# Grouped cross attention of a decoder: one pipeline over sixteen half sequences, with split float32r products

## The reference

```python
q = (x @ Wq).reshape(B, S, 16, 128)          # x: 8 x 256 x 512, Wq: 512 x 2048
k = (ctx @ Wk).reshape(B, S_enc, 4, 128)     # ctx: 8 x 256 x 512, Wk, Wv: 512 x 512
v = (ctx @ Wv).reshape(B, S_enc, 4, 128)
q = rms_norm(q, q_norm_w)                    # per head, eps 1e-6
k = rms_norm(k, k_norm_w)
k, v = repeat(k, 4), repeat(v, 4)            # four query heads share a key head
scores = einsum('bqhd,bkhd->bhqk', q, k) / 128 ** 0.5
out = einsum('bhqk,bkhd->bqhd', softmax(scores), v)
x = layernorm(x + out.reshape(B, S, 2048) @ Wo)
```

## Time and profile before

| | us |
|---|---|
| median of 3 runs (lowest, highest) | 3929.01 (3926.07, 3935.84) |
| span of the profiled execution | 3915.1 |
| PE busy, matmuls, in the span | 3308.1 (84%) |
| DVE, ACT, POOL busy | 1672.6 (43%), 1159.5 (30%), 238.9 (6%) |
| mean granted TensorE clock | 0.943 of full |

### The profile page before, as it was taken

How to read it: one execution, slowest core, us unless ns; L and a number is a source line. 1 busy time by engine, 2 the same in 40 slices (tenths; PEclk the granted TensorE clock), 3 DMA queues, 4 the chain that set the end, 5 groups by cost and what they waited for, 6 DMA issues and landing times. The chain is left out here.

```text
span 3915.1 us, 45980 instructions
## 1 busy us (share of the span) xinstructions
PE 3308.1 (84%) x15122; PEld 1924.5 (49%) x15123; DVE 1672.6 (43%) x3287; ACT 1159.5 (30%) x3024; POOL 238.9 (6%) x205
## 2 busy tenths in 40 slices
PE   6999667788876699999788878999999998799894
PEld 5666412222221567777555545555665555444441
DVE  5666646666665212112166653333443333211113
ACT  2333224445444111111044433323343332211110
POOL 1000100000000200000100000000000001300002
PEclk9999879989898799999899999999999999999997
DMA  1000264444440300000100003000000000700323
GB/s 65 22 16 17 58 89 76 71 70 70 70 70 27 104 17 17 12 11 17 41 14 28 23 31 115 17 17 11 7 17 17 12 6 26 271 17 32 118 78 113
DMA packets 113094, 186.93 MB, mean 48 GB/s; under 512 B 8840, under 2 KB 53352, under 8 KB 112912
## 3 DMA queue, kind: packets, MB, share of 16 engines
q1 hardware_dynamic: 92032, 135.40, 14.3%
q0 software_dynamic: 7664, 27.40, 2.0%
q10 hardware_dynamic: 13216, 21.82, 1.6%
HBM read 130.10 MB, written 54.10 MB: 47 GB/s over the span
## 5 line engine op out<-in xcount | busy, mean ns | idle before, releaser
L1143 DVE TENSOR_REDUCE x_minus_max<-banks 128x2 f32<-128x1024 f32 x256 | 308.6, 1221 | 176.4 <-PE banks L1251 173.3
L1088 ACT ACTIVATE x_probs<-banks 128x512 f32<-128x512 f32 x512 | 290.9, 596 | 278.8 <-PE banks L1269 206.1
L1269 PE MATMUL banks<-x_stacked_q,x_stacked_k 105*128 105x512 bf16 x512 | 207.9, 416 | 83.0 <-ACT x_probs L1088 59.8
L476 ACT ACTIVATE a_probs<-banks,a_minus_max 128x128 f32<-128x128 f32 (+1 forms) x512 | 209.0, 426 | 145.0 <-DVE a_minus_max L559 143.3
L1984 PE MATMUL banks<-x_w_q,x_xT 128*128 128x512 f32 x512 | 232.6, 600 | 17.3 <-ACT x_xT L1856 17.3
L1251 PE MATMUL banks<-x_stacked_k,x_stacked_q 102*128 102x512 bf16 x512 | 171.5, 420 | 85.3 <-DMA x_stacked_k<-x_mask_parts_dram 60.5
L2090 PE MATMUL banks<-x_w_o,x_ctxT 128*128 128x512 f32 x512 | 221.0, 592 | 0.0
L1880 ACT ACTIVATE x_probs<-banks,x_minus_max,x_rroot 128x256 f32<-128x256 f32 x256 | 142.3, 560 | 204.1 <-DVE x_minus_max L1941 204.1
L1269 PEld LDWEIGHTS banks<-x_stacked_q,x_stacked_k 105*128 105x128 bf16 x512 | 50.4, 100 | 302.4 <-ACT x_probs L1088 194.0
L559 DVE TENSOR_REDUCE a_minus_max<-banks 128x2 f32<-128x512 f32 (+1 forms) x192 | 131.7, 686 | 82.3 <-PE banks L709 62.2
L2421 DVE TENSOR_TENSOR m_h<-banks,m_silu 128x512 f32<-128x512 f32 x39 | 27.0, 692 | 318.7 <-PE banks L2537 166.6
(11 more groups left out here) (347 smaller groups left out, 6431.9 us busy)
## 6 DMA issues: line engine op xcount, KB each, us to landing
x_parts_dram<-x_parts SPq DMA_DIRECT2D x16, 768.0 KB, 9.2
x_stacked_q<-x_parts_dram SPq DMA_DIRECT2D x48, 256.0 KB
x_stacked_k<-x_parts_dram SPq DMA_DIRECT2D x48, 256.0 KB
x_after<-a_z SPq DMA_DIRECT2D x16, 512.0 KB, 2.8
x_x<-x_after SPq DMA_DIRECT2D x16, 512.0 KB, 5.4
x_after<-x_z SPq DMA_DIRECT2D x16, 512.0 KB, 2.9
m_w<-in_m_g SPq DMA_DIRECT2D x8, 1024.0 KB, 5.7
m_w<-in_m_u SPq DMA_DIRECT2D x8, 1024.0 KB, 9.0
```

The source lines that it names most:

```text
L476: ins = act.activation(probs[:, n % 3, i * width:(i + 1) * width], psum[uses.bank(use)][:, i * width:(i + 1) * width], ACT.Exp, bias=minus ...
L1088: act.activation(probs[:, n % 8, :], psum[at.bank(f"exp{n}")], ACT.Exp, scale=SCALE)\
L1143: dve.tensor_reduce(minus_max[:, c % 2, h % 4, 2 * (n % 2):2 * (n % 2) + 2], at.pair(use), AX.X, ALU.max, negate=True)\
L1269: ins = pe.matmul(psum[at.bank(use)], stacked[1][u][:, h, s * P:(s + 1) * P], stacked[0][u][:, h, :], start=True, stop=True)
```

## The change

The stage is written anew as one pipeline over 16 units: first heads 0 to 7 of all eight sequences, then heads 8 to 15 of all eight. The first pass stores `x` plus its half of y to a scratch tensor (`half_way`), the second adds its half to that, normalises and stores. So `x` and the context are loaded and transposed twice. A period of the pipeline has eight steps, one for each head of its own unit (`own`); between the heads stand the y of the unit before (`prev`, yA0, yA1 for its heads 0 to 3 and yB0, yB1 for 4 to 7) and the projections of the next (`next`: xT, k, q, kT, qT). The table `grouped_schedule` sets the order for PE, ACT and DVE alike. S has PSUM banks 2 and 3, T 4 and 5, O 6 and 7, and everything else shares banks 0 and 1.

Every product of the stage becomes a split one. Each operand is therefore rounded by ACT (`high_part_act`) and its rest is taken by DVE from PSUM; the context's parts are POOL's (`split_context`). Weights come in 20 pieces of 512 KB (`LOADS_AT`), each rounded by ACT and its rest taken by DVE at a place of its own (`SPLITS_AT`). R, `x_spread` and `x_inverse_rows` go; instead POOL multiplies the softmax by the inverse sums (`normalise`) ahead of T. T comes three steps behind S, and O four. `release_semaphores` is called ahead of the stage.

```diff
@@ cross_attention_grouped (before: L1710 to L2092) @@
...
-                    for j in range(2):
-                        use = f"xT{j}.{u}"
...
-                            for t in range(TT):
-                                ins = pe.transpose(psum[uses.bank(use)][:, t * P:(t + 1) * P], inverse_rows[:, h % QUEUE, t, :], core.ident[:, :])
...
+def high_part_act(act, out, x):
+    return act.copy(out.bitcast(F32R), x)
...
+def grouped_schedule(prev, own, following):
...
+    steps = []
+    for n in range(HH):
+        step = []
+        if own:
+            step.append(("S", "own", n))
+        early = {0: [("qT0_1", "own"), ("v", "own")], 1: [("q1_0", "own")], 2: [("q1_1", "own")], 3: [("qT1_0", "own"), ("xT1", "next")],
+                 4: [("yB0", "prev")], 5: [("q0_0", "next")], 6: [("q0_1", "next")], 7: [("qT0_0", "next")]}
+        late = {0: [("kT1", "own")], 1: [("yA0", "prev")], 2: [("xT0", "next"), ("yA1", "prev")], 3: [("k", "next")],
+                4: [("qT1_1", "own")], 5: [("yB1", "prev")], 6: [("kT0", "next")], 7: []}
+        step += [(what, whose, None) for what, whose in early[n]]
+        step.append(("T", "own", n - T_LAG) if n >= T_LAG else ("T", "prev", n + HH - T_LAG))
+        step += [(what, whose, None) for what, whose in late[n]]
+        step.append(("O", "own", n - O_LAG) if n >= O_LAG else ("O", "prev", n + HH - O_LAG))
+        there = {"prev": prev, "own": own, "next": following}
+        steps.append([item for item in step if there[item[1]]])
+    return steps
...
+    banks = {"qT0_1": 0, "v": 1, "kT1": 0, "q1_0": 1, "yA0": 0, "q1_1": 1, "xT0": 0, "yA1": 1, "qT1_0": 0, "xT1": 1, "k": 0,
+             "yB0": 1, "qT1_1": 1, "q0_0": 0, "yB1": 1, "q0_1": 0, "kT0": 1, "qT0_0": 1}
+    rings = {"S": 2, "T": 4, "O": 6}
...
+    def every_unit(engine, period):
+        period(Period(before_first, 0, None, None, -1, -1, None, 1, 0), False, False, True)
...
+            def run(uses, turn, pair, last, last_turn):
+                w = pair * 2
+                b = w - B * half
+                first, end = (isinstance(w, int) and w == 0), (isinstance(w, int) and w + 2 == UNITS_IN_ALL)
+                period(Period(uses, turn, last, last_turn, w, b, pair, 0, half), not first, True, True)
+                period(Period(uses, turn, uses, turn, w + 1, b + 1, pair, 1, half), True, True, not end)
+            run(opening, 0, TURNS * half, last, last_turn)
+            with engine.Fori(0, TURNS - 2) as turn:
+                run(looped, turn, turn + (TURNS * half + 1), looped, turn - 1)
+            run(closing, 0, TURNS * half + TURNS - 1, looped, TURNS - 3)
+            last, last_turn = closing, 0
+        period(Period(after_last, 0, last, last_turn, UNITS_IN_ALL, B, UNITS_IN_ALL // 2, 0, HALVES - 1), True, False, False)
...
+        raw = sb("raw", [P, 2, PIECE])
+        w_kv = [sb(f"w_kv_{part}", [P, 2, KC, GH * HD]) for part in ("high", "rest")]
+        w_q = [sb(f"w_q_{part}", [P, GH, KC, HG * HD]) for part in ("high", "rest")]
+        w_o = [sb(f"w_o_{part}", [P, HH, D]) for part in ("high", "rest")]
...
+        LOADS_AT = {(-1, 0): [4, 5], (0, 0): [6, 7], (0, 1): [8, 9], (6, 0): [10, 11], (6, 1): [12], (7, 1): [13, 14, 15, 16, 17],
+                    (8, 1): [18, 19]}
+        SPLITS_AT = {(-1, 7): [4, 5], (0, 1): [6], (0, 3): [7], (0, 5): [8], (0, 7): [9], (6, 4): [10], (7, 1): [11], (7, 2): [12],
+                     (7, 3): [13], (7, 4): [14], (7, 6): [15], (8, 4): [16], (8, 5): [17], (8, 7): [18], (9, 0): [19]}
...
+            def split_context(w, c):
+                high_part(pool, ctx_parts[0][:, c, :], context[:, c, :]).then_inc(context_rounded, 1)
+                pool.wait_ge(context_rounded, w * KC + (c + 1))
+                subtract(pool, ctx_parts[1][:, c, :], context[:, c, :], ctx_parts[0][:, c, :]).then_inc(context_split, 1)
+            def normalise(w, s):
+                pool.wait_ge(inverse_ready, w * HH + (s + 1))
+                pool.tensor_tensor(probs[:, s % 4], probs[:, s % 4], inverse[:, s, :].unsqueeze(2).broadcast_to([P, TT, S1]), ALU.mult)\
+                    .then_inc(normalised, 1)
...
+            def round_piece(k):
+                act.wait_ge(raw_loaded[k % 2], (k // 2 + 1) * 16)
+                if k >= 18:
+                    act.wait_ge(z_added, B)
+                high_part_act(act, piece_of(0, k), raw[:, k % 2, :]).then_inc(w_rounded, 1)
...
+                def exps(s):
+                    bank = psum[bank_of(x_now, f"S{s}", u)]
+                    act.wait_ge(max_ready, w * HH + (s + 1))
+                    for t in range(TT):
+                        at = (s % HG) * TT + t
+                        ins = act.activation(probs[:, s % 4, t, :], bank[:, t * S1:(t + 1) * S1], ACT.Exp,
+                                             bias=minus_max[:, s, t:t + 1], scale=rroot[:, 1 + s // HG, at:at + 1],
+                                             accum_out=sums[:, s, t:t + 1])
+                    ins.then_inc(free[bank_of(x_now, f"S{s}", u)], 1)
...
+                        elif what == "T":
+                            wait_full(f"T{h}", of)
+                            high_part_act(act, probsT[0][:, h % 2], psum[bank_of(x_now, f"T{h}", of)][:, :].rearrange("p (s t) -> p s t", s=TT))\
+                                .then_inc(probs_rounded, 1)
...
+                            wait_full(f"O{h}", of)
...
+                            high_part_act(act, ctxT[0][:, h, :], psum[bank_of(x_now, f"O{h}", of)][:, 0:T]).then_inc(ctx_rounded, 1)
+                        elif what == "k":
+                            square(what, of, of_w * 5)
...
+            def rest_of_piece(k):
+                dve.wait_ge(w_rounded, k + 1)
+                subtract(dve, piece_of(1, k), raw[:, k % 2, :], piece_of(0, k)).then_inc(w_split, 1)
...
+                            dve.wait_ge(probs_rounded, of_w * HH + (h + 1))
+                            subtract(dve, probsT[1][:, h % 2], psum_of(f"T{h}", of)[:, :].rearrange("p (s t) -> p s t", s=TT), probsT[0][:, h % 2])\
+                                .then_inc(free_of(f"T{h}", of), 1)
+                        elif what == "O":
+                            dve.wait_ge(ctx_rounded, of_w * HH + (h + 1))
+                            subtract(dve, ctxT[1][:, h, :], psum_of(f"O{h}", of)[:, 0:T], ctxT[0][:, h, :]).then_inc(free_of(f"O{h}", of), 1)
...
+                    if n == 4 and following:
+                        dve.wait_ge(rroot_ready, (w + 1) * 3 + 1)
+                        dve.tensor_tensor(k_rows[:, :, :].rearrange("p t (g d) -> p (t g) d", g=GH),
+                                          psum_of("k", 1 - u)[:, :].rearrange("p (a d) -> p a d", a=4),
+                                          rroot[:, 0, 0:4].unsqueeze(2).broadcast_to([P, 4, HD]), ALU.mult).then_inc(free_of("k", 1 - u), 1)
+                        wait_free("k", 1 - u)
+                        dve.sem_inc(k_scaled, 1)
+                    if own:
+                        use = f"S{n}.{u}"
+                        dve.wait_ge(free[x_now.bank(use)], x_now.count(use) + 2)
+                        dve.reciprocal(inverse[:, n, :], sums[:, n, :]).then_inc(inverse_ready, 1)
+                    if n == 7 and prev and norm_rows:
+                        normalise_rows(1 - u)
+                    for k in placed(SPLITS_AT, w, n):
+                        rest_of_piece(k)
...
+                        wait_bank(label, of)
...
+                            for t in range(TT):
+                                ins = split_matmul(pe, out[:, t * S1:(t + 1) * S1], [part[:, g, h % HG, t * P:(t + 1) * P] for part in qT],
+                                                   [part[:, g, :] for part in kT], start=True, stop=True)
+                        elif what == "T":
+                            pe.wait_ge(normalised, of_w * HH + (h + 1))
...
+                        elif what == "O":
+                            if h == HH - O_LAG:
+                                wait_free_in_last(f"T{h}", of)
+                            else:
+                                wait_free(f"T{h}", of)
+                            if h == 0:
+                                pe.wait_ge(v_split, of_w + 1)
+                            g = h // HG
+                            for k in range(TT):
+                                ins = split_matmul(pe, out[:, 0:T], [part[:, of, k, g * HD:(g + 1) * HD] for part in v],
+                                                   [part[:, h % 2, k, :] for part in probsT], start=k == 0, stop=k == TT - 1)
...
+                        core.release_semaphores()  @@ decoder_layers, ahead of the stage @@
```

More of the change, by code:

```diff
@@ L1706 @@
 S1 = 256
[L1707 to L1733 removed]
+HALVES = 2
@@ L1772, in cross_attention_grouped @@
[L1772 to L1775 removed]
+        x = sb("x", [P, TT, D])
+        z = sb("z", [P, 2, TT, D])
+        context = sb("context", [P, KC, S1])
+        ctx_parts = [sb(f"context_{part}", [P, KC, S1]) for part in ("high", "rest")]
```

(2 more changed lines are left out.)

741 lines of the change are left out of this document (432 added, 309 removed).

## The result

The changed kernel takes 3939.76 us (median of 16 runs, 3927.34 to 3955.80) against 3924.80 for the kernel before in the same sets of runs: a ratio of 1.0042, interval 1.0030 to 1.0054. That is 15 us slower where I had forecast no change. The profiled execution has a span of 3936.6 us.

The account below looks back on a forecast made before the run. PE's own work was taken to bound the stage; the 166 us saved went back to waits, clock, boundary and split weights, summing to 977 us against 978.5. Hence 3927 us, no change, range 3858 to 3972.

Parts of the forecast that it names:

- boundary: Ahead of the stage: clearing 65 semaphores, the usual gap between blocks and a further barrier, 9 us.
- to the first S: Before the first unit: four weight pieces one behind the other, then xT, k, k_rows, q, qT, 31 us.
- last unit and tail: Stage's end: last unit without successor, the last y (15.5 us) and its normalisation (4.6), 63 us together.
- two waits for a qT: In each period PE waits 2.95 us for k in step 3 and 2.8 at the next unit's first S.
- the small ones: Shorter PE waits in a period: kT1 0.35, yA1 0.45, qT1_1 0.5, q0_0 1.05 us, among others.
- The clock's term of 1.8 us: Per period, one and a half clock falls of 1.4 us, less 0.35 absorbed; 27 us over 15 units.
- the slower rival: Clock falls behind both long waits, 3.4 us a period instead of 1.8: 3951 us, chance 0.28.
- the weights' 20 us: Second half's weights: ten splits on DVE, each up to 2.5 us, plus a late load in unit 7.
- 2.7 us of normalisation: Second half, each period: DVE's row statistics and two normalising instructions between units, making 57.2 us a period.
- The lock: POOL's normalise holds x_minus_max on DVE through their shared SBUF ports, 2.0 us of waits a period.
- the pair of ends: Start before the first unit, 31 us, and last unit with its y and normalisation, 63 us.
- The faster rivals: Shorter chains, no lock or clock loss: 3870 us, chance 0.32; PE stays the bound, waits vanish: 3750, chance 0.06.

Follow-up runs that it names:

- e5: Changed kernel with three transposes of q (qT1_0, qT0_0, qT0_1) moved ahead of S in steps 3, 7 and 0: 3870.9 us.
- e1: Changed kernel with unread identity transposes keeping PE busy, 18 ahead of k and 12 ahead of a unit's first S: 3904.4 us.
- e8: Changed kernel with a fourth pass, rest by rest, in every product of the stage: 4100.3 us, ratio 1.0461.
- e10: e9 with v also moved ahead of S of step 0: 3783.7 us, ratio 0.9632.
- e3: Changed kernel with each head's reciprocal moved behind the next head's x_minus_max: 3885.3 us, ratio 0.9909.
- e9: e5 with e3's reciprocal, bank, k_rows and load-order repairs, and weight pieces three and four split behind k before the first unit: 3799.1 us.

## Why the prediction was wrong

The sum had 977 us from store to store; the same stretch is 991 (994.7 less the 3.6 from last store to the next load, and the rows of SP after). Term by term, with the first S of units 0, 1, 9 and 15 as marks:

```profile
2395.69 0.36 PE L105 MATMUL banks<-x_kT_high,x_qT_high 128*128 128x256 f32 x1 [1.49 <-DVE x_qT_rest L98]
...
2447.58 0.35 PE L105 MATMUL banks<-x_kT_high,x_qT_high 128*128 128x256 f32 x1 [1.08 <-DVE x_qT_rest L98]
...
2919.24 0.36 PE L105 MATMUL banks<-x_kT_high,x_qT_high 128*128 128x256 f32 x1 [2.32 <-DVE x_qT_rest L98]
...
3266.18 0.40 PE L105 MATMUL banks<-x_kT_high,x_qT_high 128*128 128x256 f32 x1 [2.30 <-DVE x_qT_rest L98]
```

| term | predicted (with 1.8 of clock a unit) | measured |
|---|---|---|
| boundary | 9 | 8.4 |
| to the first S | 31 | 39.7 |
| first unit | 49.8 | 51.9 |
| units 1 to 8 with the weights | 470.4 | 471.7 |
| units 9 to 14 | 353.8 | 346.9 |
| last unit and tail | 63 | 72.5 |

- **The mechanism was right**: the 21 us a sequence that PE saves are taken back by two waits for a qT (2.95 and 2.8 us predicted; 2.72 and 2.15 to 2.2), by the small ones, and by the clock. e5 shows the long waits with the falls behind them, e1 the clock by itself, and e8 that PE's work stands in series with the waits.
- **The loop's sum was right to 6 us in 824, by errors that cancel.** The waits of a period come to 7.6 us instead of 8.9, and PE's own work to about 47.0 us (its busy time in e10's period of 48.1) instead of 45.6. The clock's term of 1.8 us was too small for the first half (e1: 2.8, near the 3.4 of the slower rival) and the weights' 20 us too large (unit 7 is some 8 us longer than its neighbours, 66.0 for 57.6 and 58.8; where the other splits went was not looked into). In the second half I added 2.7 us of normalisation to the clock's loss, but the two overlap: e1 shows 2.0 us for the one at the full clock, 0.5 beside the falls.
- **The lock** was right as a mechanism and over-priced as a wait (2.0 us a period; 0.9 by e3), while its effect on the clock was in no term.
- **The step that failed is the pair of ends**, 31 and 63 us, which measured 39.7 and 72.5: 18 us too short, more than the whole difference. To the first S I counted four weight pieces one behind the other and then `xT`; but DVE, in order, took `xT` behind the fourth piece, whose load had been asked for late, as its timeline shows:

```profile
2368.62 1.22 DVE L98 TENSOR_TENSOR x_w_q_rest<-x_raw,x_w_q_high 128x1024 fp32r<-128x1024 f32 x1 [0.99 <-ACT x_w_q_high L93]
...
2372.36 1.22 DVE L98 TENSOR_TENSOR x_w_q_rest<-x_raw,x_w_q_high 128x1024 fp32r<-128x1024 f32 x1 [2.51 <-ACT x_w_q_high L93]
...
2373.50 0.68 DVE L98 TENSOR_TENSOR x_xT_rest<-banks,x_xT_high 128x512 fp32r<-128x512 f32 x1
...
2374.24 0.58 PE L105 MATMUL banks<-x_w_kv_high,x_context_high 128*128 128x256 f32 x1 [10.07 <-DVE x_xT_rest L98]
```

From 2369.84 DVE has nothing to do for 2.51 us, until ACT's rounding of the fourth piece, and `xT`'s rest comes only at 2373.50, with PE idle for 10.07 us. e9 moves it and finds 4 of the 8.7 us. The rest is open, but the sum had its clock for the 15 units alone, and PE runs at the half clock at both ends too:

```profile
2374.24:2377.65 3.41, 3.41 (x16) 3.41 (x17) 0.67 (x1) 0.00 (x0) 0.00 (x0) 0.50 0.75 229
2382.84:2386.25 3.41, 3.41 (x9) 2.75 (x10) 0.00 (x0) 0.00 (x0) 0.00 (x0) 0.58 0.00 0
3314.00:3322.00 8.00, 6.19 (x22) 5.41 (x23) 4.34 (x8) 2.66 (x7) 1.26 (x1) 0.57 0.18 68
```

In the first two rows, behind waits of 10.07 and 3.42 us, PE is at work all through; with 0.50 and 0.42 of it lost that is 3.1 us, an estimate that no run tests. The prediction's reading that PE never waits more than a microsecond holds for the old stage's loop; at its start PE waited 12.2 and 11.7 us (ahead of 2346.90 and 2360.52).

In the last unit I let PE run its own y with no waits but those of a period. Without a next unit's projections there is nothing to cover the chain S, exponentials, normalise, T, rounding, subtraction, O, and O waits twice:

```profile
3293.89 0.55 PE L105 MATMUL banks<-x_kT_high,x_qT_high 128*128 128x256 f32 x1 [2.35 <-DVE x_qT_rest L98]
...
3311.83 0.36 PE L105 MATMUL banks<-x_probsT_high,x_v_high 128*128 128x256 f32 x1 [2.93 <-DVE x_probsT_rest L98]
...
3315.81 0.55 PE L105 MATMUL banks<-x_probsT_high,x_v_high 128*128 128x256 f32 x1 [2.59 <-DVE x_probsT_rest L98]
```

With the 2.35 us ahead of an S that is 7.9 us, and the clock behind them. No run changes the last unit by itself, so this part is read from the trace and not shown by an experiment. The 15.5 us that I gave the last y had no working either: its 48 passes of 0.230 us are 11.0.

The forecast of no change rested on 977 us against 978.5: an error of 1.5% in the one gives either sign, and my own chances had 0.46 on faster, 0.22 on the same and 0.32 on slower. That 3927 lies only 13 us under the measured time is luck in part: it stood on a median of 3929.0 from three runs of the kernel before, which is 3924.8 over sixteen. As a difference I forecast 1.5 us less and measured 15.0 more. The slower rival had its direction from the clock, which was worse than my 1.8 in the first half; but it shared the two short ends, and with them right it would have been at 3969, so it wasn't the case either. The faster rivals fell by the waits and by the lock's record.

## What to carry to other kernels

When a rewrite cuts the work of the bounding engine (here from 112 us a sequence to 91), write down for each shared bank who empties it, what stands ahead of that in each in-order queue, and how much work the first engine has meanwhile; where a head's maximum and exponentials stand ahead of an evacuation, move the evacuated product ahead of the head. In this loop TensorE's waits of 2.7 and 2.15 us cost 2.8 us a period beyond their length, by the half clock behind them, and those of 2.3 and 1.7 us far less (a mean clock of 0.99), so shortening a wait by tenths can be worth whole microseconds. And cost the first and last turn of a pipeline by their own chains; they have none of the loop's cover.
